# Storing the second norm of the expert stage as rows of factor and shift instead of as normalized images

## What is computed

```
x1 = x + attention(ln_c(x))                     # eps 1e-6, over the 128 channels
t  = tokens of x1                                # 16 x 1024 tokens of 128 numbers
xn = (t - mean(t)) / sqrt(var(t) + 1e-5)         # the second norm, over the same 128 channels
w  = softmax(mean of xn over the 16 images @ Wr + br)      # one weight per pixel and expert
h1 = relu(bn(xn @ W1[e] + b1[e]));  h2 = relu(bn(h1 @ W2[e] + b2[e]))
x2 = x1 + sum over e of w[:, e] * (h2 @ Wo[e] + bo[e])
```

## Time and profile before

| what | value |
|---|---|
| median of three runs | 807.85 us (806.77 to 808.19) |
| the profiled execution | 808.72 us, its span 806.9 us |
| TensorE busy | 786.7 us, 97% |
| GpSimd busy | 580.6 us, 72% |
| VectorE busy | 529.9 us, 66% |
| ScalarE busy | 441.1 us, 55% |
| DMA | 64.5 MB, 80 GB/s over the span |
| mean granted TensorE clock | 0.996 |

### The profile page before, as it was taken

One profiled execution on the slowest core, in us unless ns is written; L12 is line 12 of the kernel. 1 busy time (PEld: TensorE's weight loads), 2 busy tenths in 40 slices (PEclk: granted clock), 3 DMA queues, 4 the chain that ended last, 5 costly groups with the idle time before them and its releaser, 6 DMA issues.

```text
span 806.9 us, 12733 instructions
## 1 busy us (share of the span) xinstructions
PE 786.7 (97%) x4186; PEld 666.3 (83%) x4186; DVE 529.9 (66%) x1010; ACT 441.1 (55%) x550; POOL 580.6 (72%) x498
## 2 busy tenths in 40 slices
PE   5999999999999989999999999999999999999997
PEld 4898999999988668888888888888888888888885
DVE  4678787787866656565665665656656566566663
ACT  2566776767766645454554545545545455454542
POOL 5548788788786387777667777777667777777665
PEclk9999999999999999999999999999999999999999
DMA  8124334344333250120210202202012021120100
GB/s 243 53 80 155 133 128 163 127 156 156 131 132 131 68 222 30 48 79 1 78 63 15 78 0 78 78 0 78 26 52 78 0 78 40 38 78 0 52 26 26
DMA packets 22107, 64.52 MB, mean 80 GB/s; under 512 B 2608, under 2 KB 6840, under 8 KB 22080
## 3 DMA queue, kind: packets, MB, share of 16 engines
q1 hardware_dynamic: 22080, 64.19, 21.8%
HBM read 38.98 MB, written 25.20 MB: 80 GB/s over the span
## 4 chain that ended last, share of the span: by engine, by line
PE 88%; DVE 4%; DMA 2%; issue 2%; ACT 1%; SPq 1%; POOL 1%; POOLq 0%; DVEq 0%; ACTq 0%
PE psum L545 62%; PE psum L498 6%; PE psum L535 6%; PE psum L513 5%; PE psum L524 3%; DMA w_raw<-in_Wo 1%; PE psum L397 1%; PE psum L383 1%; DVE st L938 1%; DMA route_all<-route_scratch 1%; PE psum L457 1%; PE psum L458 1%; PE psum L459 1%; PE psum L371 1%; DVE rawmax L971 0%
## 5 line engine op out<-in xcount | busy, mean ns | idle before, releaser
L981 DVE SCALAR_TENSOR_TENSOR h_lo<-psum,h_hi 128x1024 fp32r<-128x1024 f32 x128 | 156.8, 1225 | 192.1 <-ACT h_hi L770 192.1
L770 ACT ACTIVATE h_hi<-psum 128x1024 fp32r<-128x1024 f32 x128 | 131.6, 1028 | 253.5 <-PE psum L545 253.1
L1141 POOL TENSOR_TENSOR h_lo<-w_raw,h_hi 128x1024 fp32r<-128x1024 f32 x64 | 154.1, 2410 | 46.7 <-ACT h_hi L782 46.7
L545 PE MATMUL psum<-h_hi,w_hi 128*128 128x512 f32 x384 | 119.5, 392 | 4.1 <-DVE w_raw L997 3.6
L545 PE MATMUL psum<-h_lo,w_hi 128*128 128x512 f32 x384 | 120.1, 394 | 0.0
L545 PE MATMUL psum<-h_hi,w_lo 128*128 128x512 f32 x384 | 119.4, 392 | 0.0
L997 DVE SCALAR_TENSOR_TENSOR w_raw<-psum,minus_t,route_all 128x1024 f32<-128x1024 f32 x93 | 118.6, 1276 | 0.7 <-PE psum L545 0.7
L1141 POOL TENSOR_TENSOR xn_lo<-w_raw,xn_hi 128x1024 fp32r<-128x1024 f32 x32 | 78.4, 2449 | 53.4 <-ACT xn_hi L782 53.4
L1141 POOL TENSOR_TENSOR xn_lo<-feat_most,xn_hi 128x1024 fp32r<-128x1024 f32 x32 | 77.1, 2411 | 51.8 <-ACT xn_hi L782 51.8
L1120 POOL TENSOR_TENSOR ln<-ln,const 128x8 f32<-128x8 f32 x32 | 52.5, 1641 | 58.8 <-DVE ln L965 58.8
L545 PEld LDWEIGHTS psum<-h_hi,w_hi 128*128 128x128 f32 x384 | 71.5, 188 | 22.6 <-issue 5.1
(11 more groups left out here) (172 smaller groups left out, 1449.7 us busy)
## 6 DMA issues: line engine op xcount, KB each, us to landing
route_all<-in_x SPq DMA_DIRECT2D x16, 512.0 KB, 3.8
x_res<-in_x SPq DMA_DIRECT2D x16, 512.0 KB, 3.2
x_scratch<-x_res SPq DMA_DIRECT2D x16, 512.0 KB, 2.8
xn_scratch<-xn SPq DMA_DIRECT2D x16, 512.0 KB, 2.6
xs_in<-xn_scratch SPq DMA_DIRECT2D x16, 512.0 KB, 4.6
x_res<-x_scratch SPq DMA_DIRECT2D x16, 512.0 KB, 3.2
out<-x_res SPq DMA_DIRECT2D x15, 512.0 KB, 2.6
route_all<-route_scratch SPq DMA_DIRECT2D x6, 512.0 KB, 6.5
```

The lines of the kernel that those rows point to most:

```text
L545: mm = pe.matmul(dst[:, px], w[:, which, e, :], part[:, px], start=first and w is w_hi and part is hi, stop=last and part is lo, skip_grou ...
L770: nc.scalar.activation(h1_hi[r][:], z1[r] if src is None else src, ACT.Relu).then_inc(h1_hi_done, 1)
L981: nc.vector.scalar_tensor_tensor(out=h1_lo[r][:], in0=z1[r] if src is None else src, scalar=0.0, in1=h1_hi[r][:].bitcast(F32), op0=ALU.max ...
L1141: nc.gpsimd.tensor_tensor(h2_lo[r][:], h2w[r], h2_hi[r][:].bitcast(F32), ALU.subtract).then_inc(h2_lo_done, 1)
```

## The change

The normalized image is no longer turned back, copied and stored. Factor and shift of an image are 16 columns of one small tensor (`ln[1]`, whose rows SHIFT and RSTD are made neighbours), and one 128x16 transpose turns them into rows (`turn_rows`, in TensorE's round between the wait for y and m). ScalarE moves the 16x128 result with a bias of 1 on the eight shift rows (`move_rows`, placed ahead of the copy `mT_hi`), and SyncE stores 8 KB. In the expert stage `xs_in` is loaded from x1 itself, a broadcast of the two rows over 128 partitions (1 MB) is loaded to `rows`, and GpSimd multiplies and adds on 128x1024 (`scale_xs` at k%8 = 1, `shift_xs` at k%8 = 3). `bias_x1` goes from k%8 = 1 to k%8 = 7. ScalarE's `xs_hi` waits for GpSimd. For image 0 both steps stand in round 14 ahead of GpSimd's statistics, for image 1 the factor stands in the bridge after `add_feature` of image 13 and the shift after the last norm. `norm2_split` is 4 for all images instead of 3 for most. In rounds 14 and 15 TensorE's order is changed around the place of the old turns. The slot loop makes one trip less, so 16 more slots are written out.

```diff
         def norm2_split(image):
-            return 4 if at(image, IMAGES - 3) or at(image, IMAGES - 1) else 3
+            return 4
...
-            trips = (SLOTS - first) // period
+            trips = (SLOTS - first) // period - 1
...
+            def load_rows(b):
+                sp.wait_ge(xs_made, b)
+                sp.dma_start(rows[:], rows_dram[b, 0:1, :].to_broadcast([128, 2 * PIXELS])).then_inc(rows_loaded, 16)
...
             def load(b, p):
                 sp.wait_ge(xs_lo_done, b - 1)
                 sp.wait_ge(xs_hi_done, b - 1)
-                sp.dma_start(xs_in[p][:], xn2_dram[b]).then_inc(xs_loaded[p], 16)
+                sp.dma_start(xs_in[p][:], x1_dram[b]).then_inc(xs_loaded[p], 16)
+                load_rows(b)
...
-                if d and not s:
-                    turn_xn2(t - 3, p_k)
+                if at(t, IMAGES - 2):
+                    turn_e(t, 0, 1)
+                if at(t, IMAGES - 1):
+                    pe.wait_ge(exp_done, 2 * IMAGES)
+                    pe.wait_ge(xs_lo_done, 1)
+                    half_layer1(p_tok, 0, 0)
...
                     pe.wait_ge(y_moved, t)
+                    if d:
+                        turn_rows(t - 3)
                     for j in range(2):
                         mm = pe.matmul(p_g[:, 256:384], wqkv_sb[:, j, :], y_sb[:, j, :], start=j == 0, stop=j == 1)
...
                 if at(t, IMAGES - 1):
-                    pe.wait_ge(exp_done, 2 * IMAGES)
-                    pe.wait_ge(xs_lo_done, 1)
-                    layer1_into(p_tok, 0)
-                if b and not at(t, 0):
+                    half_layer1(p_tok, 0, 1).then_inc(l1_done, 1)
+                if b and not at(t, 0) and not at(t, IMAGES - 2):
                     turn_e(t, 0, 1)
...
                     turn_e(t, 1, 0)
-                    if d and s:
-                        pe.wait_ge(copy1_done, t + 3)
-                        turn_xn2(t - 3, p_k)
                     add_g(t, p, 0, 1)
...
+            def turn_rows(image):
+                pe.wait_ge(ln_done[1], image + 1)
+                pe.wait_ge(ctx_moved, image + 3 if not isinstance(image, int) else min(image + 3, IMAGES))
+                wait(pe, rows_moved, image)
+                pe.transpose(p_g[0:2 * CHUNKS, 384:512], ln[1][:, SHIFT:RSTD + 1, :].rearrange("p k n -> p (k n)"),
+                             ident[:]).then_inc(rows_turned, 1)
...
                 if c:
                     act.wait_ge(m_done, t)
+                    if d:
+                        move_rows(t - 3, q)
                     wait(act, mx_done, t - 1)
                     nc.scalar.copy(mT_hi[:], p_g[:, 256:384]).then_inc(m_hi_done, 1)
...
-                    if d and s:
-                        xn2_out(t - 3, q, p_k)
                     move_e(t, 1, 1)
+                if at(t, IMAGES - 2):
+                    first_xs_high(0)
...
+            def first_xs_high(b):
+                act.wait_ge(xs_made, b + 1)
+                nc.scalar.copy(xs_hi[b][:], xs_in[b][:]).then_inc(xs_hi_done, 1)
...
             h1_high(4, 4)
-            act.wait_ge(feat_moved, 1)
-            xn2_out(IMAGES - 1, 1, p_chan)
+            first_xs_high(1)
             act.wait_ge(step_done, 3)
             nc.scalar.activation(grown[:].rearrange("p n e -> p (n e)"), shifted[:].rearrange("p n e -> p (n e)"), ACT.Exp).then_inc(grown_done, 1)
+            move_rows(IMAGES - 1, 1)
...
+            def scale_xs(b, p):
+                pool.wait_ge(xs_loaded[p], 8 * b + (8 if p else 16))
+                pool.wait_ge(rows_loaded, 16 * b + 16)
+                nc.gpsimd.tensor_tensor(xs_in[p][:], xs_in[p][:], rows[:, PIXELS:], ALU.mult).then_inc(xs_scaled, 1)
+
+            def shift_xs(b, p):
+                pool.wait_ge(xs_scaled, b + 1)
+                nc.gpsimd.tensor_tensor(xs_in[p][:], xs_in[p][:], rows[:, 0:PIXELS], ALU.add).then_inc(xs_made, 1)
...
+                if at(t, IMAGES - 2):
+                    scale_xs(0, 0)
+                    shift_xs(0, 0)
                 if f:
                     statistics(1, t - 2)
+                    if at(t, IMAGES - 2):
+                        split_low(0, 0)
...
             add_feature(IMAGES - 3)
-            split_low(1, 1)
+            scale_xs(1, 1)
             for image, tokens in ((IMAGES - 2, x1T), (IMAGES - 1, xT)):
...
+            shift_xs(1, 1)
+            split_low(1, 1)
             h2_low(0, 0)
...
             pool.wait_ge(bias_moved, 1)
-            bias_x1(0, 0)
             h2_low(3, 3)
...
+                if k % EXPERTS == 1 and exists(s + EXPERTS):
+                    scale_xs(image + 1, 1 - k // EXPERTS)
+                if k % EXPERTS == 3 and exists(s + EXPERTS):
+                    shift_xs(image + 1, 1 - k // EXPERTS)
                 if k % EXPERTS == 5 and exists(s + EXPERTS):
                     split_low(image + 1, 1 - k // EXPERTS)
-                if k % EXPERTS == 1 and exists(s):
+                if k % EXPERTS == 7 and exists(s):
                     bias_x1(image, k // EXPERTS)
```

More of the change, by code:

```diff
@@ L153, in metaformer_kernel @@
         xn2T = sb("xn2T", [128, CHUNKS, C])
-        xn2 = [sb(f"xn2_{p}", [C, PIXELS]) for p in range(2)]
+        rows_out = [sb(f"rows_out{p}", [2 * CHUNKS, 128]) for p in range(2)]
+        row_bias = sb("row_bias", [2 * CHUNKS, 1])
+        rows = sb("rows", [128, 2 * PIXELS])
         st = [sb(f"st{k}", [128, CHUNKS, 6]) for k in range(2)]
@@ L460, in add_m @@
                 mm.then_inc(mx_done, 1)
-            def turn_xn2(image, dst):
-                pe.wait_ge(norm2_first, image + 1)
-                pe.wait_ge(norm2_last, image + 1)
-                wait(pe, xn2_moved, image)
-                turn(dst, lambda n: xn2T[:, n, :]).then_inc(xn2t_done, 1)
+            def turn_rows(image):
[4 more added lines that the diff above has]
+                             ident[:]).then_inc(rows_turned, 1)
             def spread_scales(dst, col):
@@ L611, in _ @@
             pe.wait_ge(y_moved, IMAGES)
+            turn_rows(IMAGES - 3)
             for j in range(2):
@@ L624, in _ @@
             layer2(1, 1)
-            turn_xn2(IMAGES - 2, p_chan)
+            pe.wait_ge(copy2_done, IMAGES)
+            turn_rows(IMAGES - 2)
             pe.wait_ge(h1_lo_done, 2)
@@ L635, in _ @@
             pe.wait_ge(feat_most_moved, 1)
-            turn_xn2(IMAGES - 1, p_chan)
+            pe.wait_ge(norm2_first, IMAGES)
+            pe.wait_ge(norm2_last, IMAGES)
+            turn(p_chan, lambda n: xn2T[:, n, :]).then_inc(last_turned, 1)
             pe.wait_ge(h1_lo_done, 3)
@@ L717, in step @@
                     nc.scalar.copy(xn_hi[q][:], p_tok).then_inc(xn_hi_done, 1)
-                for r in range(2):
-                    if at(t, IMAGES - 2 + r):
-                        if r:
-                            h1_high(0, 0, p_tok)
-                        act.wait_ge(xs_loaded[r], 16)
-                        nc.scalar.copy(xs_hi[r][:], xs_in[r][:]).then_inc(xs_hi_done, 1)
+                if at(t, IMAGES - 1):
+                    h1_high(0, 0, p_tok)
                 if b:
                     move_e(t, 1, 0)
-                    if d and s:
-                        xn2_out(t - 3, q, p_k)
                     move_e(t, 1, 1)
+                if at(t, IMAGES - 2):
+                    first_xs_high(0)
                 if f and not at(t, IMAGES - 1):
                     act.wait_ge(ln_done[1], t - 1)
-                    wait(act, xn2t_done, t - 2)
                     wait(act, feat_done, t - 2)
@@ L792, in _ @@
             nc.scalar.copy(x1T[:], p_tok).then_inc(copy2_done, 1)
-            xn2_out(IMAGES - 3, 1, p_chan)
             act.wait_ge(m_done, IMAGES)
+            move_rows(IMAGES - 3, 1)
             act.wait_ge(mx_done, IMAGES - 1)
@@ L802, in _ @@
             z2_out(1)
-            xn2_out(IMAGES - 2, 0, p_chan)
+            move_rows(IMAGES - 2, 0)
             h1_high(2, 2)
@@ L837, in slot @@
                     p = 1 - k // EXPERTS
-                    act.wait_ge(xs_loaded[p], 8 * image + (16 if p else 24))
+                    act.wait_ge(xs_made, image + 2)
                     wait(act, l1_done, s - 4)
@@ L1036, in _ @@
             h1_low(3, 3)
[L1038 removed]
+            dve.wait_ge(last_turned, 1)
             dve.wait_ge(feat_most_moved, 1)
@@ L1119, in statistics @@
                 pool.wait_ge(var_done[k], image + 1)
+                if k == 1:
+                    wait(pool, rows_turned, image)
                 nc.gpsimd.tensor_tensor(o[:, RSTD], o[:, VARIANCE], const[:, MINUS_HALF], ALU.pow).then_inc(rstd_done[k], 1)
```

65 lines of the change are left out of this document (32 added, 33 removed).

## The result

| | before | after |
|---|---|---|
| median, us | 807.76 (4 runs) | 811.83 (4 runs, 811.38 to 813.10) |
| profiled execution, us | 808.7 | 811.38 |
| its span, us | 806.9 | 809.6 |

A forecast was written before the change was run, and what follows sets the result against it. TensorE was taken to bound the kernel, 88% of its chain. Terms -7.0 + 0.2 + 0.0 + 2.75 + 0 + 1.6 = -2.45, said as -2.5, gave 805.3 us from 807.85, range 801.7 to 809.7.

The forecast's parts named there:

- Cost 0: Expert slots: GpSimd's scale and shift fit beside TensorE's work, xs_hi with 0.4 to spare, so nothing is added.
- (c): Rival: rounds gain as said, but the clock falls twice and end and slots cost 1 or 2 more: 807.5; chance 0.15.
- The rounds: Rounds t = 4 to 13: 0.70 us gained in each of 10, -7.0, the period becoming about 13.93.
- round 3: VectorE's w_lo delays round 4's reductions, so TensorE's gain is lost and move_rows' 0.25 is not: +0.2.
- Rival (b): Rounds: VectorE's run becomes the bound through move_rows ahead of mT_hi, making the kernel slower, 811.3 at g = 0.1; chance 0.18.
- (d): Rival: GpSimd's norm waiting for TensorE's turn holds the rounds, and the bridge's costs stay: 809; chance 0.08.
- Rounds 14 and 15: VectorE's small instructions wait for GpSimd's shift, +0.8 in round 14; round 15 gains 0.76; sum 0.0.
- The bridge: 252 to 291 us, a chain through all engines: +2.75 in all, between 0.4 and 3.7.
- the lock: Bridge: VectorE's shifted, two SBUF inputs, stands still until GpSimd's 128x1024 split ends: +1.95.
- rival (a): The lock does not bite or VectorE comes first: bridge costs 0.4, rounds 14 and 15 gain 1.1, total 801.9; chance 0.17.
- the clock's term: Bridge: eight transposes in the chain take 0.9 more if TensorE's clock falls; half put in, +0.4.
- The end: Last image's bias_x1 in slot 127 delays the last two h2_low, and TensorE's last layer waits: +1.6.

The follow-up runs named there:

- after_lock: after_spacer8 with VectorE's split_low(1, 1) of the bridge moved behind h2_low(3, 3): 803.82 us, ratio to the kernel before 0.9936.
- after_spacer8: Changed kernel with the spacer ahead of xs_in 8 columns instead of 16, experts' tensors back at 192 mod 256: 803.91 us, ratio to the kernel before 0.9944.
- after_both: after_lock with the last image's bias_x1 moved to k % 8 == 1 in place of 7: 801.77 us, ratio to the kernel before 0.9926.
- after_best: after_both with the weights w_hi and w_lo at 192 mod 256 in place of 128, moving operands unmoved: 796.15 us, ratio to the kernel before 0.9863.
- after_light_pool: Changed kernel with GpSimd alone working on 8 of 1024 columns in the looped slots: 811.81 us, one execution.
- after_light_all: Changed kernel with ScalarE, VectorE and GpSimd working on 8 of 1024 columns in the looped slots (xs_hi keeps its width): 813.7 us, one execution.

## Why the prediction was wrong

**The slots: the step that failed.** "Cost 0" rested on waits and on GpSimd's room. Both readings were right: no wait of TensorE, GpSimd 85 of 100, the 0.4 that `xs_hi` should have to spare came out as 0.48. What the step took for granted was that a matmul costs what it cost before if its code is unchanged. It measured +8.43 us over 500: some 3.9 ns on each of some 2190 matmuls (500.6 / 0.2289). The price was not in any of the rivals; (c) allowed the slots and the end 1 or 2 more, by code or waits. The last sentence of the prediction, slots of 4.12 us and "if they are longer, the slots' term was wrong", is what showed it: 18 x 232.8 ns are 4.19, against 18 x 228.9 = 4.12. With placement restored the kernel takes 803.91, inside the predicted range and 1.4 below the forecast.

**The rounds.** Expected -7.0 and +0.2 in round 3, together -6.8 for rounds 3 to 13; measured -6.14. The mechanism is as told: `move_rows` 0.27 against 0.25, the 0.92 of VectorE gone, 13.92 us for a period of 13.93. But of rounds 5 to 12 only four take 13.92 to 13.94; the other four take 14.12 to 14.18. The sum had taken one period for all; with VectorE's slack at nothing, as it had itself reckoned, the rounds come out uneven. In round 3 the reverse: it became 0.97 shorter (15.55 to 14.58), round 4 after it 0.32 longer (14.59 to 14.91). Their sum, -0.65, is near the -0.5 of the prediction. Rival (b), `move_rows` as the bound, fell, and so did (d); a longer `move_rows` wasn't tried.

**Rounds 14 and 15.** Round 14 +0.52 for +0.8, round 15 -0.98 for -0.76. VectorE's first small instruction slipped in between scale and shift and the others stood until the end of shift, as told; 228.87 + some 1.5 is the 230.42 of `k_half`.

**The bridge: mechanism right, size wrong.** Expected +2.75, measured +0.76 in the changed kernel. Of its terms the lock is shown at 1.98 for 1.95, so rival (a) fell. It is seen in `shifted`, 0.22 alone (after_lock) and 2.05 beside `xs_lo`, where it ends at 269.52 and `xs_lo` at 269.44. Beside narrow instructions of GpSimd the kernel before shows no standstill: L958 at 104.23 takes 0.18 beside 128x128 chunks of `xn2T`, and `w_lo` 1.21, as each time, beside a 128x8 instruction. The step that failed is the clock's term, +0.4 for a fall behind the first stall and nothing for the second. It was an estimate, half of 0.9: eight transposes (8 x 2.78 / 24 = 0.93) that take twice as long at the 0.50 of the earlier trace rows. No run shows the 0.4. Behind TensorE's 2.16 us of idle time the clock fell to 0.50 and the 24 transposes took 4.45 instead of 2.78. But the chain hardly noticed: from the transposes' start to layer 2 of slot 5 it was 285.86 - 270.62 = 15.24 us, against 285.91 - 270.85 = 15.06 in after_spacer8, whose transposes ran at full clock, so +0.18. The rest went into TensorE's wait before layer 2 of slot 5, which shrank from 2.66 to 0.70. And the fall of the clock that the kernel before has behind that wait didn't occur: layer 2 of slot 5 to the second `xn_hi,w_hi` took 7.16 before and 5.66 after, -1.50. This term the sum had left out. In after_spacer8 the clock fell at the second stall and not at the first, and the bridge took 48.59, +2.07: the lock and 0.09 for all else. With 0.18 and -1.50 that makes the +0.76. After stalls of 2.64 to 2.67 the clock fell in before, after_spacer8 and after_lock, and stayed at 1.00 in after_both and after_best. The program alone doesn't decide this. Up to the looped slots after_light_pool and after_light_all are the changed kernel: in the first the clock fell behind the first stall (2.18), in the second it stayed at 1.00 there (2.16) and fell behind the second (2.58). And over the five executions of after_both the mean granted clock was 1.000 in two (800.09 and 800.43 us) and 0.996 to 0.998 in three (801.77 to 801.99 us). So the -1.50 was luck, and what decides between the two stays open.

**The end.** +1.28 for +1.6: the bias ahead of the last two `h2_low` as told. TensorE waits 1.12 and 0.68 where it waited 0.80. The missing 0.3 is GpSimd's: counted from TensorE's last `h_lo,w_hi`, the bias began 0.12 earlier than reckoned (797.50 - 800.55 against 796.25 - 799.18), and the instructions behind it followed at 2.37 and 2.33 us instead of 2.4.

**What holds without the slots.** By the table -1.20 of the 2.7 is the start of this execution. The stretches other than that and the slots give -6.14 - 0.46 + 0.76 + 1.28 + 0.03 = -4.5, where -2.5 was forecast; 1.5 of the gain is the bridge's second stall at full clock, which was luck. With the experts' tensors back in their old place the kernel is 3.6 us quicker than the one before (803.91 against 807.53, ratio 0.9944, 0.9904 to 0.9984). The change does what it says, and as a piece of scheduling it gains.

## What to carry to other kernels

When a change adds, removes or resizes a tensor, list where the operands of the matmuls start before and after, and treat it as a term of the sum: here it was 8 us in 500, larger than all else that the change did. A count of matmuls in a stretch without waits is the test, and a spacer of 32 to 256 bytes the remedy; try a few placements of weights and moving operands when a kernel is bound by TensorE. And where two stalls hang on one chain, price them together: here time that the first stall added was taken off the wait at the second.

## What the runs showed of the hardware

Pace of a 128x512 fp32r matmul in gapless stretches at a granted clock of 1.00, averaged over a kernel's slots from start to start: 226.7 ns (442 or 443 in 100 us), 228.9 or 229.0 (438, 439) or 232.2 to 233.3 (430 to 433), set by where the weights and the moving operand start in SBUF, and 232.8 in the changed kernel as in after_light_all, where the three other engines are busy for 7 to 10 of 100 us. With distance (moving minus weights) 0 or 64 mod 256 it was 226.7 to 229.0, with 32, 96, 128, 192 and 224 it was 232.2 to 233.3; 160 wasn't tried. The pace belongs to the single block of matmuls: moving `h2_` alone made its blocks 233.1 instead of 228.9. What causes this stays open. VectorE's small instructions with SBUF inputs stood still beside GpSimd's 128x1024 instructions in the three cases shown of the changed kernel (L975 1.19 beside the product, L979 2.23 beside the sum, `shifted` 2.05 beside the difference, against 0.17, 0.17 and, in after_lock, 0.22 alone). The granted clock of TensorE fell to 0.50 behind an idle time of 2.16 us in after and stayed at 1.00 behind the same in after_spacer8; behind 2.64 us it fell to 0.50 in after_lock and stayed at 1.00 in after_both.
